# First three trees routed by matrix products: nodes on partitions, an ancestor matrix, one-hot leaves

## The reference, cut to what matters

```
node = jnp.zeros(x.shape[:2], dtype=jnp.int32)
for _ in range(DEPTH):
    logit = jnp.einsum('bsd,bsd->bs', x, nw[node]) + nb[node]
    node = 2 * node + 1 + (logit > 0).astype(jnp.int32)
leaf = node - NN
h = act(jnp.einsum('bsd,bsdl->bsl', x, w1[leaf]) + b1[leaf])
return jnp.einsum('bsl,bsld->bsd', h, w2[leaf]) + b2[leaf]
```

## Time and profile before

| what | value |
|---|---|
| time, median of 3 runs | 716.09 us (713.92 to 716.23) |
| the profiled execution, its own time | 716.28 us |
| its span in the trace | 714.6 us |
| mean granted clock of TensorE | 0.942 of full |
| busy: PE, DVE, ACT, POOL | 81%, 62%, 47%, 36% of the span |

### The profile page before, as it was taken

How to read it: one execution, slowest core, us unless ns; L and a number is a source line. 1 busy time by engine, 2 the same in 40 slices (tenths; PEclk the granted TensorE clock), 3 DMA queues, 4 the chain that set the end, 5 groups by cost and what they waited for, 6 DMA issues and landing times.

```text
span 714.6 us, 11516 instructions
## 1 busy us (share of the span) xinstructions
PE 576.0 (81%) x3540; PEld 413.1 (58%) x3540; DVE 441.7 (62%) x1024; ACT 336.8 (47%) x738; POOL 255.1 (36%) x242
## 2 busy tenths in 40 slices
PE   2276644799999999999999898998976898989930
PEld 0164532577777777776767655656643466666620
DVE  2959987657576666666667556555768565555300
ACT  5520001455555545464646554545223378878720
POOL 4401766750006578267003820000000776000285
PEclk9998758899999999999999999999999799999985
DMA  7979541275657778788551210000000357445123
GB/s 222 253 170 218 215 134 44 54 198 154 163 148 207 195 196 164 184 186 188 155 160 42 34 16 15 1 1 1 0 1 0 112 111 168 133 134 143 41 34 76
DMA packets 108828, 83.42 MB, mean 117 GB/s; under 512 B 8688, under 2 KB 105840, under 8 KB 108768
## 3 DMA queue, kind: packets, MB, share of 16 engines
q1 hardware_dynamic: 93472, 70.07, 37.0%
q0 software_dynamic: 15104, 12.63, 9.6%
q10 hardware_dynamic: 192, 0.00, 0.0%
HBM read 58.30 MB, written 24.36 MB: 116 GB/s over the span
## 4 chain that ended last, share of the span: by engine, by line
PE 59%; DVE 8%; issue 5%; ACT 5%; POOL 4%; DMA 0%; POOLq 0%; DVEq 0%; ACTq 0%
PE ps L983 8%; PE ps L960 7%; PE ps L971 7%; PE ps L973 7%; PE ps L1037 7%; PE ps L1047 6%; POOL xr L386 3%; PE ps L943 3%; DVE ps L618 2%; PE ps L1090 2%; PE ps L1042 2%; ACT hr L797 2%; PE ps L1031 2%; PE ps L998 1%; PE ps L1097 1%
## 5 line engine op out<-in xcount | busy, mean ns | idle before, releaser
L618 DVE CUSTOM_DVE_ANT_0 ps<-ps,strip 128x512 f32<-128x512 f32 x256 | 176.9, 701 | 132.7 <-PE ps L960 128.4
L786 ACT ACTIVATE pt<-ps 128x512 f32<-128x512 f32 x256 | 150.7, 600 | 91.1 <-PE ps L973 89.4
L381 POOL DMA_INDIRECT xs<-xr,slot x64 | 63.4, 990 | 244.6 <-issue 154.8
L971 PE MATMUL ps<-qs,km 128*128 128x512 f32 x256 | 127.1, 497 | 8.4 <-ACT pt L786 7.5
L960 PE MATMUL ps<-km,qs 128*128 128x512 f32 x256 | 111.8, 443 | 15.9 <-DVE mx L618 7.4
L386 POOL DMA_INDIRECT yt<-ys,slot x48 | 74.6, 1555 | 80.5 <-DMA ys<-yl 66.5
L797 ACT ACTIVATE hr<-ps,wt 128x128 f32<-128x128 f32 x192 | 54.7, 368 | 68.0 <-PE ps L1037 68.0
L973 PE MATMUL ps<-u_lo,rev_r 128*128 128x220 f32 (+1 forms) x256 | 74.5, 291 | 0.0
L973 PE MATMUL ps<-u_hi,rev_r 128*128 128x220 f32 (+1 forms) x256 | 73.2, 286 | 0.0
L983 PE MATMUL ps<-pt,v_aug 128*32 128x512 f32 x512 | 69.0, 612 | 0.7 <-ACT pt L786 0.7
L971 PEld LDWEIGHTS ps<-qs,km 128*128 128x128 f32 x256 | 49.0, 191 | 31.2 <-ACT pt L786 19.6
(11 more groups left out here) (207 smaller groups left out, 864.2 us busy)
## 6 DMA issues: line engine op xcount, KB each, us to landing
wt<-in_wl SPq DMA_DIRECT2D x192, 128.5 KB, 2.4
xl<-xs SPq DMA_DIRECT2D x48, 258.0 KB
ys<-yl SPq DMA_DIRECT2D x48, 256.0 KB
xs<-mx SPq DMA_DIRECT2D x2, 3096.0 KB, 23.7
strip<-bias_bf SPq DMA_DIRECT2D x1, 3584.0 KB, 36.2
u_hi<-bias_hi SPq DMA_DIRECT2D x1, 2496.0 KB, 16.1
u_lo<-bias_lo SPq DMA_DIRECT2D x1, 2496.0 KB, 28.5
xs<-xr,slot POOLq DMA_INDIRECT x64
```

The lines of the kernel that those rows point to most:

```text
L381: pool.indirect_dma_start(out=xs[t % 2][:, :], out_offset=bass.IndirectOffsetOnAxis(ap=slot[:, t, k:k + 1], axis=0), in_=xr[:, k, :], in_o ...
L618: V.tensor_tensor_reduce(out=bank(u % banks), in0=bank(u % banks), in1=strip[:, HG * g + j, b0:b0 + NS], scale=1.0, scalar=LOWEST, op0=ALU ...
L786: A.activation(pt[:, kt % 2, j, :], bank(2 + u % 2), ACT.Exp).then_inc(S["ex"], 1)
L971: T.matmul(bank(2 + u % 2), km[:, par, j, kt * P:(kt + 1) * P], qs[:, par, :], start=True, stop=False)
```

## The change

Trees q, k and v are routed in another form; tree f is left as it was (`decide` and `ranked` are the two halves of the old `route`).

- **Logits with nodes on partitions.** Node vectors are stationary (128 nodes at a time), 512 tokens are moving; a chunk is 512 tokens, 4 chunks a tree, 12 in all, two banks each (`logits`).
- **Bits** are one DVE comparison a bank with a bias per partition (`bits_of`), written as bf16 with nodes on partitions.
- **Ancestor matrix.** PE multiplies the bits by a 256 x 256 matrix of -1, 0 and +1 (`paths`): four bf16 products a chunk give, for each leaf, how well the bits match the way to it (`follow`). ACT's Relu with a bias per leaf (`pop`) leaves a one-hot over leaves.
- **Block matrix.** PE multiplies the one-hot (128 tokens stationary) by a matrix with 32 block columns and one column of leaf numbers (`settled`): 8 products of 33 columns a chunk. DVE copies the blocks and the leaf numbers (`places`). `ranks` and the tail `ranked` stay, with tokens on partitions.
- **The matrices are made on the chip**, by 50 POOL instructions (`tree_rows`), placed between the addition to `acc` and `left_rows`; PE waits for them (`tc`) before its first product. Four short products, a transpose of the biases and two DVE instructions make the Relu bias and the negated biases (`pop`).
- **Loads.** The biases come as 8 rows of 512 bytes in place of 768 values on every partition (384 KB written).
- **Order.** PE's loop runs the chunks in a pipeline: `logits(i)`, `follow(i-1)`, `settled(i-2)`; tree t's `ranks` stand behind the logits of the third chunk of tree t+1, and DVE's `ranked` behind that chunk's bits. ACT sends the first block list behind its first chunk of tree v, the other two behind the evictions of the attention's values.

```diff
+LOGIT_BANKS = ((2, 3), (4, 5))
+PATH_BANKS = (6, 7)
+CELL = LEAVES // 8 + 1
+CHUNKS = 4
...
             sp.dma_start(nodes[:, 0:NTREE * NODES].rearrange("p (a n) -> p a n", n=NODES), nw[:, 0:NTREE, :]).then_inc(S["d_n"], 16)
-            sp.dma_start(nodes[:, NTREE * NODES:2 * NTREE * NODES].rearrange("p (a n) -> p a n", n=NODES),
-                         bass.AP(tensor=nb.tensor, offset=0, ap=[[0, P], [NODES, NTREE], [1, NODES]])).then_inc(S["d_n"], 16)
+            sp.dma_start(nb_rows, bass.AP(tensor=nb.tensor, offset=0, ap=[[P, 2 * (NTREE + 1)], [1, P]])).then_inc(S["d_n"], 16)
...
+            def tree_rows():
+
+                n1, wd, first, mid, end, one = (tcs[:, i, :] for i in range(6))
+                for h in range(2):
+                    settle(G.tensor_scalar(n1[:, h:h + 1], cst[:, C_T:C_T + 1], 1.0 / P, float(P * h + 1), ALU.mult, ALU.add))
+                settle(G.memset(wd, float(LEAVES)))
+                for lv in range(1, 8):
+                    settle(G.tensor_scalar(one, n1, float(1 << lv), -float(1 << (8 - lv)), ALU.is_ge, ALU.mult))
+                    settle(G.tensor_tensor(wd, wd, one, ALU.add))
...
+                row, tmp, low = ks[:, 0:LEAVES], ks[:, LEAVES:2 * LEAVES], ks[:, LEAVES:LEAVES + BLK]
+                b8 = cst[:, C_B8:C_B8 + BLK]
+                for r in range(LB):
+                    settle(G.tensor_scalar(row.rearrange("p (j r) -> p j r", r=LB)[:, :, r], b8, float(r), None, ALU.add))
+                for h in range(2):
+                    settle(G.tensor_scalar(paths[:, h], row, mid[:, h:h + 1], 2.0, ALU.is_ge, ALU.mult))
+                    for edge in (first, end):
+                        settle(G.tensor_scalar(tmp, row, edge[:, h:h + 1], None, ALU.is_ge))
+                        settle(G.tensor_tensor(paths[:, h], paths[:, h], tmp, ALU.subtract))
...
+                pool.sem_inc(S["tc"], 1)
...
             nc.gpsimd.tensor_tensor(acc[:], acc[:], bpb.unsqueeze(1).to_broadcast([P, NT, P]), ALU.add).then_inc(S["wsc"], 1)
+            tree_rows()
             left_rows()
...
+            def bits_of(i):
+
+                t, c = divmod(i, CHUNKS)
+                for h in range(2):
+                    dve.wait_ge(S["lg"], 2 * i + h + 1)
+                    V.tensor_scalar(bitsT[:, h, c * NS:(c + 1) * NS], bank(LOGIT_BANKS[i % 2][h]), nbT[:, t, h:h + 1], None,
+                                    ALU.is_gt).then_inc(S["bit"], 1)
+
+            def places(t, work):
+
+                cells = ps[:, 0:2, 0:NT // 2 * CELL].rearrange("p a (t n) -> p a t n", n=CELL)
+                dve.wait_ge(S["hb"], t + 1)
+                V.tensor_copy(work.bitcast(BF16)[:, 30 * NT:62 * NT].rearrange("p (a t n) -> p a t n", a=2, n=BLK),
+                              cells[:, :, :, 0:BLK])
+                then(V.tensor_scalar(leaf[:, t, :].rearrange("p (a t) -> p a t", a=2), cells[:, :, :, BLK], float(LEAVES * t), None,
+                                     ALU.add))
+                dve.sem_inc(S["oh5"], 1)
...
+            for i in range(NTREE * CHUNKS + 3):
+                if i < NTREE * CHUNKS:
+                    bits_of(i)
+                t, c = divmod(i, CHUNKS)
+                if c == 1 and t > 0:
+                    places(t - 1, t1)
+                if c == 2 and t > 0:
+                    for _ in ranked(t - 1, t1, (0, 1)):
+                        pass
...
+            for i in range(NTREE * CHUNKS):
+                t, c = divmod(i, CHUNKS)
+                if c == 1 and t == 2:
+                    tile_blocks(0)
+                for h in range(2):
+                    act.wait_ge(S["pa"], 2 * i + h + 1)
+                    A.activation(leafT[:, h, c * NS:(c + 1) * NS], bank(PATH_BANKS[h]), ACT.Relu, bias=pop[:, h:h + 1]
+                                 ).then_inc(S["oh"], 1)
...
+            def logits(i):
+
+                t, c = divmod(i, CHUNKS)
+                if i >= 2:
+                    pe.wait_ge(S["bit"], 2 * i - 2)
+                for h in range(2):
+                    T.matmul(bank(LOGIT_BANKS[i % 2][h]), nws[t][:, h * P:(h + 1) * P], xn2T[:, c * NS:(c + 1) * NS],
+                             start=True, stop=True).then_inc(S["lg"], 1)
+
+            def follow(i):
+
+                c = i % CHUNKS
+                pe.wait_ge(S["bit"], 2 * i + 2)
+                if i > 0:
+                    pe.wait_ge(S["oh"], 2 * i)
+                for h in range(2):
+                    for k in range(2):
+                        last = T.matmul(bank(PATH_BANKS[h]), paths[:, k, h * P:(h + 1) * P], bitsT[:, k, c * NS:(c + 1) * NS],
+                                        start=k == 0, stop=k == 1)
+                    last.then_inc(S["pa"], 1)
+
+            def settled(i):
+
+                t, c = divmod(i, CHUNKS)
+                pe.wait_ge(S["oh"], 2 * i + 2)
+                if c == 0 and t > 0:
+                    pe.wait_ge(S["rt"], t)
...
+            pe.wait_ge(S["tc"], 1)
...
+            pe.wait_ge(S["pop"], 2)
+            for i in range(NTREE * CHUNKS + 3):
+                if i < NTREE * CHUNKS:
+                    logits(i)
+                t, c = divmod(i, CHUNKS)
+                if c == 2 and t > 0:
+                    ranks(t - 1, t1, (0, 1))
+                if 1 <= i <= NTREE * CHUNKS:
+                    follow(i - 1)
+                if 2 <= i <= NTREE * CHUNKS + 1:
+                    settled(i - 2)
```

More of the change, by code:

```diff
@@ L364, in far_rows @@
                 pool.sem_inc(S["aug"], 1)
+            def tree_rows():
[6 more added lines that the diff above has]
+                    settle(G.tensor_tensor(wd, wd, one, ALU.add))
+                settle(G.tensor_tensor(first, n1, wd, ALU.mult))
+                settle(G.tensor_scalar(first, first, -float(LEAVES), None, ALU.add))
+                settle(G.tensor_tensor(end, first, wd, ALU.add))
+                settle(G.tensor_scalar(wd, wd, 0.5, None, ALU.mult))
+                settle(G.tensor_tensor(mid, first, wd, ALU.add))
+                row, tmp, low = ks[:, 0:LEAVES], ks[:, LEAVES:2 * LEAVES], ks[:, LEAVES:LEAVES + BLK]
[7 more added lines that the diff above has]
+                        settle(G.tensor_tensor(paths[:, h], paths[:, h], tmp, ALU.subtract))
+                settle(G.tensor_scalar(n1, n1, -1.0, None, ALU.add))
+                settle(G.tensor_scalar(wd, n1, -float(LB), None, ALU.add))
+                for h in range(2):
+                    settle(G.tensor_scalar(blks[:, h, 0:BLK], b8, n1[:, h:h + 1], None, ALU.is_le))
+                    settle(G.tensor_scalar(low, b8, wd[:, h:h + 1], None, ALU.is_le))
+                    settle(G.tensor_tensor(blks[:, h, 0:BLK], blks[:, h, 0:BLK], low, ALU.subtract))
+                    settle(G.tensor_copy(blks[:, h, BLK:BLK + 1], n1[:, h:h + 1]))
+                pool.sem_inc(S["tc"], 1)
             def left_rows():
@@ L515, in _, with decide @@
             dve.wait_ge(S["ones"], 2)
-            def route(t, nbv, bits, work, where, rank):
+            def decide(t, nbv, bits, work, where):
                 wb = work.bitcast(BF16)
@@ L561, in route, with ranked @@
                 yield
+            def ranked(t, work, rank):
+                here = work.bitcast(BF16)[:, 30 * NT:62 * NT].rearrange("p (t n) -> p t n", n=BLK)
                 dve.wait_ge(S["rk"], t + 1)
@@ L588, in route @@
                 dve.sem_inc(S["id"], 1)
[L590 to L596, removed]
+            def bits_of(i):
[12 more added lines that the diff above has]
+                dve.sem_inc(S["oh5"], 1)
+                then(V.tensor_scalar(whole[:, 0:NT], leaf[:, t, :], LB - 1, None, ALU.bitwise_and))
+            dve.wait_ge(S["pop"], 1)
+            then(V.tensor_scalar(nbT[:].rearrange("p t h -> p (t h)"), ps[:, PATH_BANKS[0], 2:2 + 2 * (NTREE + 1)], -1.0, None,
+                                 ALU.mult))
+            V.tensor_scalar(pop[:], ps[:, PATH_BANKS[0], 0:2], -0.5, -3.0, ALU.mult, ALU.add).then_inc(S["pop"], 1)
+            for i in range(NTREE * CHUNKS + 3):
[7 more added lines that the diff above has]
+                        pass
             def split_q(n, par):
@@ L666, in route_y @@
                 yield
-                yield from route(TF, nb_f, bits_f.bitcast(BF16)[:, 0:NT * NODES].rearrange("p (t n) -> p t n", n=NODES), work_f,
-                                 [(k, FB[k % 2]) for k in range(8)], FB)
+                yield from decide(TF, nb_f, bits_f.bitcast(BF16)[:, 0:NT * NODES].rearrange("p (t n) -> p t n", n=NODES), work_f,
+                                  [(k, FB[k % 2]) for k in range(8)])
+                yield from ranked(TF, work_f, FB)
             def attention(k, i):
@@ L757, in tile_blocks @@
                 act.dma_start(ew[0:1, t * TILES:(t + 1) * TILES], ewc[0:TILES, t:t + 1]).then_inc(S[f"d_ew{t}"], 16)
[L759 to L764, removed]
+            act.wait_ge(S["pop"], 2)
+            for i in range(NTREE * CHUNKS):
[6 more added lines that the diff above has]
```

(28 more changed lines are left out.)

14 lines of the change are left out of this document (11 added, 3 removed).

## The result

The changed kernel takes **725.58 us** (median of 4 runs, 724.76 to 726.85) against 715.8 (713.92 to 716.23, 4 runs): a ratio of 1.0145, 95% interval 1.0122 to 1.0167. It is slower, by 9.8 us; 724.5 was forecast. Its profiled execution took 726.85 us, span 724.5, clock 0.947.

What follows compares the result with a forecast made beforehand. The first tree's scatter release bounds the end: 49.4 + 1.0 + 22.4 + 3.7 = 76.5 against 68.05, 8.4 us later. 716.28 + 8.4 = 724.7, 0.2 above the median, so 724.5 us; range 719.5 to 731.5.

Steps and rivals of the forecast that it cites:

- The bound: Routing stage: scatters pace the second and third tree, so only the first release, 68.05 us, can move the end.
- Step 1, matrices at 49.4: POOL's 50 `tree_rows` instructions: matrices ready at 49.4 us, being 44.2 undisturbed plus 5.2 for DVE's disturbance.
- The rival of dear comparisons: POOL's comparisons cost 0.97 us or more: matrices at 54.6 or later, time 730 to 735; chance 0.17.
- POOL not held: POOL's short instructions slip between DVE's: matrices at 44 to 45, time 719 to 720; chance 0.08.
- The walk: Stepping both queues forward on paper: DVE's L504 held about 2.3 us, tokens at 45.0, and 1.7 added to POOL.
- Not slower: Matrices ready before the tokens, PE starting at 42.7 at full clock: 715.4 us; chance 0.06.
- Steps 2, 3 and 4: First tree: short preparation 1.0 us, PE up to the counts 22.4, DVE's tail to the release 3.7.
- step 3: PE up to the first tree's counts: 19.8 us at full clock plus 2.6 lost to a slow restart, 22.4.

Runs made afterwards that it cites:

- addition later: Changed kernel with POOL's 2048-column addition to acc moved behind the 50 instructions of `tree_rows`: 720.41 us, ratio 1.010.
- matrices first: Changed kernel with `tree_rows` moved to the front of POOL's work, right behind the instruction that releases the bias table: 712.57 us, ratio 0.9972.
- `id` early: Changed kernel with DVE's wait for the scatter split off, so trees 2 and 3 raise `id` without waiting: 709.01 us, ratio 0.9927.
- logits first: Changed kernel with PE multiplying the first two chunks' logits before it waits for the matrices: 720.46 us, ratio 1.0081.
- before, addition later: Kernel before the change with only POOL's 2048-column addition moved behind `left_rows`: 712.0 us, ratio 0.9959.
- the control with both moves: Kernel before the change with POOL's addition behind `left_rows` and `id` raised ahead of the wait for the scatter: 704.55 us, ratio 0.9876.
- the two old-form kernels above: Kernel before the change with POOL's addition behind `left_rows`, 712.0 us, and the same with `id` also ahead of the scatter wait, 704.55 us.

## Why the prediction was right, and which terms were off

*The bound* held as read: the first release moved the end. It came 10.6 late (8.4 forecast); the two scatters behind it, which I had taken as fixed, gave 1.3 back; and the main stage moved by 9.35 with its length nearly unchanged. That the time came within 1.1 us of the forecast owes something to luck: the first release was 2.15 later than forecast, and the scatters hid over half of that. The experiments show it from both sides: sooner matrices move all (addition later, matrices first), and taking the scatters off the way of `id` brings the hidden savings out (`id` early).

*Step 1, matrices at 49.4*: 51.45 in the trace, 2.05 late, as a sum of misses. The six comparisons cost 6.1, not 2.7 (+3.4): I priced them at 0.45 by the memset's row, because I read most of L361's 1.46 us as a hold. That reading was right: the same cast takes 0.50 in matrices first (0.36 by my reading). But a cast is no price for a comparison, which takes 0.92 to 1.17 on fewer columns; that these lie near my upper bound of 0.97, drawn from the held row, is chance. The 32-column work cost 4.5 undisturbed, not 3.5 (+1.0; twelve have one input and take 0.32 to 0.37, while the 0.25 of the earlier trace rows is an addition of two, and the two of that kind, L405, do take 0.24), the waits about 0.08 instead of 0.07 each (+0.7), short ones +0.15, additions 2.7 instead of 2.9 (-0.2). The start was 0.6 sooner, and what DVE held was 2.0 beside L498 (2.21 for 0.22), 0.75 within L394 and about 0.1 more, 2.8, not 5.2 (-2.4); the 1.7 that I added for DVE's short instructions was hardly there. Large errors of opposite sign met: that the total was nearer than its terms is luck.

*The rival of dear comparisons* was thus true of the price, without its time: the smaller hold gave 2.4 us back. *POOL not held* was wrong, as the 2.21 beside 2.29 shows; the Trainium skill, "SBUF — State Buffer", section "Who interferes with whom", says that of two such instructions the one that issues first keeps the shared ports for its whole length and that the order decides who blocks, and the trace agrees: L385 had started before L498 and took its 0.20, the next one, L384, took 2.21 and ended 0.08 behind L498.

*The walk's claim that the norms are held by about 2.3* was wrong: L548 started at 35.39 against 35.89 before, the tokens were ready at 42.2 against 42.7. POOL's instructions of 0.2 hardly hold DVE. It cost the forecast nothing, because POOL was later, as I had said.

*Not slower* put the best that this form can do at 715.4. Matrices first measured 712.57, because the tokens, which I had taken as fixed at 42.7, came at 39.0 once the addition was out of the norms.

*Steps 2, 3 and 4* held: 1.2 from the last matrix instruction (51.45 to 52.63; 1.0 forecast), 22.4 (52.63 to 75.01) and 3.6. In step 3 the slow restart cost 2.4 (6.08 against the 3.70 in logits first; 2.6 forecast), and a chunk takes 2.87 on PE with no gaps (3.1 forecast).

*What I had in the rows and did not use*: L452's 3.52 us beside POOL's addition. I read it as proof of a hold and priced only what the new code would suffer. It was also a loss of 3.35 us that stood in the kernel already, and each of the three places tried for that addition took it away.

*Still open*: the span grew 0.55 us more than the first eviction moved, within the spread of runs; and whether the matrices are better made by DVE or loaded was not tried.

## What to carry to other kernels

When a faster step stands in front of a paced resource (here a scatter of 22 us a tree), ask first which signal waits for that resource without needing it: splitting `id` from the scatter's wait took 16.6 us off the changed kernel and 7.4 off the old form, and made the new form's gain visible. A row of another operation is a weak price, even when it is read rightly: the cast was held, as I had said, and the comparison was still twice as dear as I made it; where no row of the same operation exists, the bounds belong wide. A long instruction on POOL is worth looking at in the other engine's rows: an instruction on 8 columns that takes 3.5 us is a gain waiting to be taken.

## What the runs showed of the hardware

- **DVE was held long only by a long instruction of POOL.** POOL's addition (4.52 us) held an 8-column step of DVE for 3.35 us, in the kernel before and in the changed one; 29 us of POOL's short ones beside DVE's norms (matrices first) held DVE by some 0.8 us in all, against the same instructions of "before, addition later": 0.30 at most in one (L540, 0.47 for 0.17), 0.24 in L548.
- **The scatters ran a little faster without the level walk beside them.** In the trace of before three of scatter 0's 16 issues took 1.42, 1.15 and 1.14 in place of 0.96, just while DVE ran two-input bf16 instructions of the level walk, and four of scatter 1's took 0.98 to 1.15; the control with both moves shows the same at the same lines of the walk. In the changed kernel, whose DVE is at work there too but without the walk, all but the first of the 32 issues take 0.95 to 0.97. That is 0.8 and 0.5 us, against 0.7 and 0.56 by which the two stretches got shorter (22.88 to 22.18, 22.92 to 22.36). The cause is read from the coincidence and was not tested; other issues beside such instructions took 0.96 too.
- **The same start can be slow or fast.** In the two old-form kernels above PE has the same work up to the first logits, and starts them at 39.46 and 39.71; the granted clock of 40 to 42 us was 0.50 in the one and 1.00 in the other, these logits took 8.95 and 7.14, and the first release came 24.7 and 23.0 behind the tokens. So 1.8 us between two profiled executions can be the clock alone.
- **The clock column can lag.** In the windows of the changed kernel the restart shows 1.00, while the records of the logits there take 0.76 each where those of logits first take 0.46:

```profile
54.00:56.00 2.00, 2.00 (x3) 0.67 (x2) 0.75 (x1) 0.00 (x0) 0.00 (x0) 1.00 0.99 200
```

The same products in matrices first, 5.62 for the x8, show 0.50 for 40 to 44 us. Where this column and the durations of equal products differ, the durations were the better guide here.
